# Attention logits of two graph-attention layers: the lookup matmuls in f32 instead of on three bf16 pieces

## The chip, the cores and the metric

The program runs on one core of one Trainium2 chip. The metric is the device time of one execution in microseconds (us); less is better. A profiled execution gives, beside its time, the start and length of every instruction on each engine: TensorE (PE for the matmuls, PEld for the loads of their stationary operand), VectorE (DVE), ScalarE (ACT), GpSimd (POOL) and SyncE (SP), and the clock that TensorE was granted, as a share of 2.4 GHz.

## The reference

The reference is a chain of four graph layers over 6250 nodes, 100000 edges and 128 features: a graph attention network of two attention layers, a GCN, a relational attention and a gated graph layer, each followed by a residual addition and a layer norm. What matters here is the score of an edge in each of the two attention layers:

```python
g = h @ W
s = (g * a_src).sum(-1)
d = (g * a_dst).sum(-1)
e = jax.nn.leaky_relu(s[src] + d[dst], NEG_SLOPE)
```

`s` and `d` are one number per node. For each edge, one of `s` must be looked up by its source and one of `d` by its destination, all in f32.

## The kernel before, in words

The nodes are stored as a table of 128 partitions by 52 columns (`NBP` = 52): node n lies in partition n mod 128 (its low digit) and in column n div 128 (its high digit). `scol` and `dcol` are the two tables `s` and `d` in that form, f32. The edges go in 196 groups (`GROUPS`) of 512 (`GE`), a group in 4 tiles (`GT`) of 128 edges.

`gat_logits(l)`, called once for each of the two layers, looks up both tables for all edges. For one group:

- ACT fetches the low digits of the group's destinations and sources as a row of bf16, spread over all partitions (`g_lo_rows`, L1075, a ring of 4).
- One-hots of the low digits, 128 partitions by 512 edges for each table: DVE makes that of the destinations with one comparison (`onehot`, L1108), ACT that of the sources with a Square and a Relu (L1081, L1083). They lie in `g_oh`, bf16, a ring of 4.
- PE multiplies, for each table and tile, the one-hot (stationary, 128x128) with the table (moving, 128x52): the row of 52 candidates of each edge (L1189). The table was split ahead into three bf16 pieces that add up to the f32 number (`g_parts`, L1150 and L1154), so there are 3 matmuls for each table and tile, added up in PSUM: 24 for a group. The result lies in one of two PSUM buffers (`g_psc`).
- DVE picks the candidate of the high digit: a comparison of a column number with the high digit (`match`, L1114), a product with the candidates (`take`, L1121), a sum over the 52 columns (`choose`, L1125), and the sum of both tables (`add`, L1129, into `tmp`).

The order is written out by hand. On DVE the step for group g is: one-hot of g+2, take of g+1, add of g, match of g+2, choose of g+1. PE waits, for a group, for both one-hots (`s_oh`, `s_oh2`) and until DVE has taken the group two before out of the same PSUM buffer (`s_take`). DVE and ACT wait with a one-hot of a ring place until PE is through with the group four before (`s_c`). ACT asks for the next digits after DVE's one-hot of the same ring place (`s_oh`).

Beside it, and with no data in common, POOL gathers rows of the layer's table by indirect DMA, four transfers for a group of edges (`keep_gathers`, L264), and SP loads their indices (L268) and stores them (L272). That is 78 groups' worth in layer 0 and 76 in layer 1 (`KEPT`), the rest being gathered in other stages. The stage ends when POOL, SP and the lookups are all through; then comes the softmax over the edges of a node.

Two other places in the kernel run f32 matmuls that the prediction reads: L706 makes the logit tables of layer 0 (a transposed block of `x`, 128x128, by two columns, `w_sd`), with the transposes of L700 between; L1626 is the weighted sum over the edges (a one-hot by 131 columns).

Of the kernel before, what the change touches and what calls it, by code (L numbers as in the profile page):

```python
# [24 lines left out]
BF16 = mybir.dt.bfloat16  # L25
ALU = mybir.AluOpType
# [3 lines left out]
P = 128  # L30
# [5 lines left out]
NBP = QUADS * 4  # L36
NPAD = NBP * P
GT = 4
GE = GT * P
# [11 lines left out]
RING = 4  # L51
# [37 lines left out]
def build(nc, A, out):  # L89
    top = ExitStack()  # L90
    with top:
        def sb(stack, name, shape, dt=F32):
            return stack.enter_context(nc.sbuf_tensor(name, shape, dt))

        def ps(stack, name, shape, dt=F32):
            return stack.enter_context(nc.psum_tensor(name, shape, dt))
# [3 lines left out]
        def sem(stack, name):  # L100
            s = stack.enter_context(nc.semaphore(name))
            used.append(s)
            return s

        @contextmanager
        def phase():

            with ExitStack() as st:
                used.clear()
                yield st  # L110
                with nc.Block() as block:
                    @block.gpsimd
                    def _(pool):
                        for s in used:
                            pool.sem_clear(s)
# [5 lines left out]
        acc = sb(top, "acc", [P, NBP * D + 8])  # L121
# [901 lines left out]
        def gat_logits(l):  # L1023
# [3 lines left out]


            with phase() as st:
                part = sb(st, f"g{l}_parts", [P, 2, 3, NBP], BF16)  # L1030
                rest = sb(st, f"g{l}_rest", [P, 2, NBP])
                trow = sb(st, f"g{l}_lo_rows", [P, RING, 2 * GE], BF16)
                oh = sb(st, f"g{l}_oh", [P, RING, 2 * GE], BF16)
                pid = sb(st, f"g{l}_pid", [P, 1])
                neg_pid = sb(st, f"g{l}_neg_pid", [P, 1])
                sq = acc[:, 0:2 * GE].rearrange("p (k e) -> p k e", k=2)
# [3 lines left out]
                u = tmp[:, 0:TILES]  # L1040
                ps_c = [ps(st, f"g{l}_psc{i}", [P, 2 * GT, 64]) for i in range(2)]
                s_pid = sem(st, f"g{l}_pid_ready")
                s_part = sem(st, f"g{l}_parts_ready")
                s_lo = [sem(st, f"g{l}_lo{k}") for k in range(RING)]
                s_oh = sem(st, f"g{l}_onehot_ready")
                s_oh2 = sem(st, f"g{l}_onehot2_ready")
# [9 lines left out]
                tabs = (dcol, scol)  # L1056
                with nc.Block() as block:
                    @block.gpsimd
                    def _(pool):
                        nc.gpsimd.iota(pid_i[:, :], pattern=[[0, 1]], base=0, channel_multiplier=1).then_inc(s_pid, 1)  # L1060
                        pool.wait_ge(s_pid, 1)
                        nc.gpsimd.tensor_copy(pid[:, :], pid_i[:, :]).then_inc(s_pid, 1)
                        pool.wait_ge(s_pid, 2)
                        keep_gathers(pool, gat_src(l), last - first, k_idx, k_land, k_st)
# [36 lines left out]
                    @block.vector  # L1101
                    def _(dve):
                        v = nc.vector

                        def onehot(g, k, r):
                            dve.wait_ge(s_lo[k % RING], r * 16 + 16)
                            dve.wait_ge(s_c, g + 1)
                            v.tensor_scalar(oh[:, k % RING, 0:GE], trow[:, k % RING, 0:GE], pid[:, :], None, ALU.is_equal).then_inc(s_oh, 1)  # L1108

                        def match(g, k):  # L1110

                            hi = hi_g[:, :, bass.ds(g * GT, GT)].unsqueeze(3).to_broadcast([P, 2, GT, NBP])
                            dve.wait_ge(s_pick, g + 1)
                            v.tensor_tensor(eq[:, k % 2, :, :, :], iota[:, 0:NBP].unsqueeze(1).unsqueeze(1).to_broadcast([P, 2, GT, NBP]), hi,  # L1114
                                            ALU.is_equal).then_inc(s_eq, 1)

                        def take(g, k):
                            cand = ps_c[k % 2][:, :, 0:NBP].rearrange("p (a t) b -> p a t b", a=2)
                            dve.wait_ge(s_c, g + 1 + RING)
                            dve.wait_ge(s_eq, g + 1)  # L1120
                            v.tensor_tensor(eq[:, k % 2, :, :, :], eq[:, k % 2, :, :, :], cand, ALU.mult).then_inc(s_take, 1)  # L1121

                        def choose(g, k):
                            dve.wait_ge(s_take, g + 3)
                            v.tensor_reduce(pick[:, k % 2, :, :], eq[:, k % 2, :, :, :], AX, ALU.add).then_inc(s_pick, 1)  # L1125

                        def add(g, k):
                            dve.wait_ge(s_pick, g + 3)
                            v.tensor_tensor(u[:, bass.ds(g * GT, GT)], pick[:, k % 2, 0, :], pick[:, k % 2, 1, :], ALU.add).then_inc(s_u, 1)  # L1129

                        def body(i, k, has):
                            g = i * RING + k
                            if has(2):
                                onehot(g + 2, k + 2, i + (k + 2) // RING)
                            if has(1):
                                take(g + 1, k + 1)
                            add(g, k)
                            if has(2):
                                match(g + 2, k + 2)
                            if has(1):  # L1140
                                dve.wait_ge(s_u, g + 1)
                                choose(g + 1, k + 1)

                        dve.sem_inc(s_take, 2)
                        dve.sem_inc(s_pick, 2)
                        n = 0
                        for a, tab in enumerate(tabs):
                            left = tab[:, :]
                            for i in range(3):
                                v.tensor_copy(part[:, a, i, :], left).then_inc(s_part, 1)  # L1150
                                n += 1
                                dve.wait_ge(s_part, n)
                                if i < 2:
                                    v.tensor_tensor(rest[:, a, :], left, part[:, a, i, :], ALU.subtract).then_inc(s_part, 1)  # L1154
                                    n += 1
                                    dve.wait_ge(s_part, n)
                                    left = rest[:, a, :]
                        dve.sem_inc(s_oh, RING)
                        dve.wait_ge(s_pid, 2)
                        for g in range(LEAD):  # L1160
                            onehot(g, g, 0)
                            match(g, g)
                        take(0, 0)
                        choose(0, 0)
                        whole = (GROUPS - LEAD) // RING
                        for i in range(0, whole):
                            for k in range(RING):
                                body(i, k, lambda d: True)
                        for g in range(whole * RING, GROUPS):
                            body(g // RING, g % RING, lambda d: g + d < GROUPS)  # L1170
                        dve.wait_ge(s_u, GROUPS)
                        v.tensor_copy(gx[:, 2, :], w_g[:, :]).then_inc(s_u, 1)
                        v.scalar_tensor_tensor(gx[:, 0, :], u[:, :], SLOPE, u[:, :], ALU.mult, ALU.max).then_inc(s_u, 1)
                        dve.wait_ge(s_u, GROUPS + 2)

                    @block.tensor
                    def _(pe):
                        pe.sem_inc(s_c, RING)
                        pe.wait_ge(s_part, 10)
                        for i in range(0, GROUPS // RING):  # L1180
                            for k in range(RING):
                                g = i * RING + k
                                pe.wait_ge(s_oh, g + 1 + RING)
                                pe.wait_ge(s_oh2, g + 1 + RING)
                                pe.wait_ge(s_take, g + 1)
                                for a in range(2):
                                    for t in range(GT):
                                        for n in range(3):
                                            m = nc.tensor.matmul(ps_c[k % 2][:, a * GT + t, 0:NBP], oh[:, k, a * GE + t * P:a * GE + (t + 1) * P],  # L1189
                                                                 part[:, a, n, :], start=(n == 0), stop=(n == 2))  # L1190
                                m.then_inc(s_c, 1)

        def segment_softmax(name, x, heads, last_max=None, aside=None, kept=None):
# [1605 lines left out]
        with ExitStack() as spare:  # L2799
            rest = sb(spare, "q_rest", [P, 2, 4, D])  # L2800
# [35 lines left out]
```

## Time and profile before

| what | value |
|---|---|
| median of 3 runs | 8215.74 us (8201.44 to 8236.54) |
| the profiled execution | 8222.3 us |
| its span, first to last instruction | 8220.5 us |
| mean granted TensorE clock | 0.654 of 2.4 GHz |
| busy in the span: PE, PEld | 4066.6 us (49%), 3274.5 us (40%) |
| busy in the span: DVE, ACT, POOL | 3569.6 us (43%), 1528.5 us (19%), 4158.7 us (51%) |
| L1189, matmuls / loads | x9408, 505.7 us / 439.3 us busy |

Durations of PE are those of a pipeline: instructions of one engine overlap, so the time that one of them costs is read from the distance of the starts or from the time of a run of them, not from its own duration. "issue" as a releaser is time in which an engine waited for nothing that the profile shows. The two stages at issue lie, from the span's start, at about 292 to 1082 us (layer 0) and 1756 to 2535 us (layer 1).

### The profile page before, as it was taken

To read this page: it belongs to the slowest core of one execution; us is meant where nothing else is said; L and a number is where in the kernel's file an instruction comes from. 1 tells how busy PE (TensorE), PEld (TensorE's weight loads), DVE (VectorE), ACT (ScalarE), POOL (GpSimd) and SP (SyncE) were. 2 spreads that over 40 slices of the span, in tenths; PEclk is the share of its full clock that TensorE was granted. 3 is DMA by queue.
4 is the path that set the end of the run, shared out by engine and by line. 5 is a ranking of instruction groups with operands and counts; after the bars stand their busy time and mean duration, and the time that the engine had idled before them with its cause. 6 is when DMAs were issued, how large, how long until landed. Compare 5 with 4: busy or idle time off the path is not lost. (4 is left out here: it accounts for less than half of the span.)

```text
span 8220.5 us, 107944 instructions
## 1 busy us (share of the span) xinstructions
PE 4066.6 (49%) x29332; PEld 3274.5 (40%) x29332; DVE 3569.6 (43%) x11001; ACT 1528.5 (19%) x3905; POOL 4158.7 (51%) x4416
## 2 busy tenths in 40 slices
PE   2403635430263532334444568888888474333446
PEld 1302525430253532333344445556666363233333
DVE  3004945430395532423333455555555792122224
ACT  0003710010272000200000133333333112000003
POOL 6473045547304566466565444455454435666660
PEclk7555557765555865655555678888888796555668
DMA  5233436533343654345555244444444461111110
GB/s 143 74 103 105 146 118 177 172 113 104 102 146 115 192 154 125 89 121 139 140 150 148 66 125 137 136 141 142 139 143 136 103 184 49 46 44 43 45 44 17
DMA packets 705868, 948.48 MB, mean 115 GB/s; under 512 B 263142, under 2 KB 367103, under 8 KB 704719
## 3 DMA queue, kind: packets, MB, share of 16 engines
q1 hardware_dynamic: 405027, 408.02, 16.6%
q0 software_dynamic: 140576, 316.92, 15.1%
q10 hardware_dynamic: 159712, 216.63, 8.6%
q8 instruction: 290, 4.75, 0.2%
q14 instruction: 263, 2.15, 0.1%
HBM read 705.34 MB, written 235.74 MB: 114 GB/s over the span
## 5 line engine op out<-in xcount | busy, mean ns | idle before, releaser
L2465 POOL DMA_INDIRECT s_rows<-rel_tab,s_idx x832 | 800.5, 962 | 792.0 <-issue 770.8
L264 POOL DMA_INDIRECT stash<-in_x,src_slot x784 | 796.2, 1016 | 760.4 <-DMA src_slot<-src_g 513.6
L264 POOL DMA_INDIRECT stash<-gat_tab,src_slot x784 | 788.1, 1005 | 757.1 <-DMA src_slot<-src_g 518.6
L1189 PE MATMUL g_psc<-g_parts,g_oh 128*128 128x52 bf16 x9408 | 505.7, 220 | 1066.7 <-issue 806.8
L959 POOL DMA_INDIRECT gcn_rows<-gcn_tab,src_slot x784 | 754.5, 962 | 494.3 <-issue 225.9
L959 POOL DMA_INDIRECT ggn_rows<-ggn_tab,src_slot x784 | 749.5, 956 | 441.0 <-issue 227.3
L1626 PE MATMUL e_psb<-tmp,e_oh 128*128 x3328 | 580.7, 340 | 783.5 <-DVE e_oh L1597 528.1
L1189 PEld LDWEIGHTS g_psc<-g_parts,g_oh 128*128 128x128 bf16 x9408 | 439.3, 120 | 1133.6 <-issue 854.4
L1626 PEld LDWEIGHTS e_psb<-tmp,e_oh 128*128 128x128 f32 x3328 | 524.1, 243 | 840.4 <-issue 840.1
L1959 PE MATMUL ggn_pso<-ggn_rows,ggn_oh 128*128 x1952 | 466.3, 397 | 663.2 <-DVE acc L1896 306.6
L2128 PE MATMUL gcn_pso<-gcn_rows,gcn_oh 128*128 x1952 | 500.1, 432 | 577.8 <-issue 398.9
L1959 PEld LDWEIGHTS ggn_pso<-ggn_rows,ggn_oh 128*128 128x128 f32 x1952 | 380.0, 281 | 750.0 <-issue 749.9
L2128 PEld LDWEIGHTS gcn_pso<-gcn_rows,gcn_oh 128*128 128x128 f32 x1952 | 423.6, 317 | 610.9 <-issue 610.3
L1121 DVE TENSOR_TENSOR g_eq<-g_eq,g_psc 128x416 f32<-128x416 f32 x392 | 231.6, 591 | 836.5 <-DMA src_slot<-src_g 412.3
L1896 DVE TENSOR_TENSOR acc<-acc,ggn_pso 128x128 f32 x244 | 69.9, 287 | 941.4 <-DMA s_oh<-oh_dram 623.8
L1081 ACT ACTIVATE acc<-g_lo_rows,g_neg_pid 128x512 f32<-128x512 bf16 x392 | 282.9, 722 | 1013.2 <-issue 810.2
L2072 DVE TENSOR_TENSOR acc<-acc,gcn_pso 128x128 f32 x244 | 70.1, 287 | 822.2 <-DMA src_slot<-src_g 543.3
L1595 DVE COPY tmp<-gx 128x12 f32<-128x12 f32 x392 | 74.6, 190 | 735.8 <-DMA e_values<-edge_v 306.0
L2597 PE MATMUL s_psk<-w_kv,s_msgT 128*128 128x128 f32 x1664 | 308.5, 342 | 0.0
L2537 DVE TENSOR_TENSOR tmp<-s_psk,tmp 128x512 f32<-128x512 f32 x208 | 143.1, 688 | 360.8 <-issue 311.7
L1597 DVE TENSOR_TENSOR e_oh<-iota,drel_v 128x512 f32<-128x512 f32 x416 | 284.6, 685 | 19.7 <-PE e_psb L1626 19.7
L2597 PEld LDWEIGHTS s_psk<-w_kv,s_msgT 128*128 128x128 f32 x1664 | 261.2, 239 | 62.2 <-issue 62.2
(499 smaller groups left out, 8373.5 us busy)
## 6 DMA issues: line engine op xcount, KB each, us to landing
edge_v<-stash SPq DMA_DIRECT2D x392, 256.0 KB
g_lo_rows<-lo_rows ACTq DMA_DIRECT2D x392, 256.0 KB
e_values<-edge_v SPq DMA_DIRECT2D x392, 256.0 KB
oh_dram<-tmp ACTq DMA_DIRECT2D x208, 256.0 KB
s_oh<-oh_dram SPq DMA_DIRECT2D x208, 256.0 KB
edge_v<-acc SPq DMA_DIRECT2D x208, 256.0 KB
r_values<-edge_v SPq DMA_DIRECT2D x208, 256.0 KB, 3.0
tmp<-drel_rows ACTq DMA_DIRECT2D x208, 128.0 KB
```

The source lines that it names most:

```text
L264: pool.indirect_dma_start(stash[:, k, t, :], None, tab[:, :], bass.IndirectOffsetOnAxis(ap=src_slot[:, k, t:t + 1], axis=0)).then_inc(s_la ...
L959: pool.indirect_dma_start(rows[:, k, t, :], None, tab[:, :], bass.IndirectOffsetOnAxis(ap=src_slot[:, k, t:t + 1], axis=0)).then_inc(s_row ...
L1081: nc.scalar.activation(sq[:, k % 2, :], trow[:, k, GE:2 * GE], ACT.Square, bias=neg_pid[:, :]).then_inc(s_sq, 1)
L1121: v.tensor_tensor(eq[:, k % 2, :, :, :], eq[:, k % 2, :, :, :], cand, ALU.mult).then_inc(s_take, 1)
L1189: m = nc.tensor.matmul(ps_c[k % 2][:, a * GT + t, 0:NBP], oh[:, k, a * GE + t * P:a * GE + (t + 1) * P], part[:, a, n, :], start=(n == 0), ...
L1597: v.tensor_tensor(oh[:, k % RING, :, :], iota[:, :].unsqueeze(1).to_broadcast([P, GT, P]), drel_v[:, bass.ds(n * GT, GT)].unsqueeze(2).to_ ...
L1626: nc.tensor.matmul(ps_b[:, bass.ds(bank, 1), 0:WCOLS].rearrange("p o d -> p (o d)"), oh[:, k, t, :], wv[:, bass.ds(slot, 1), :].rearrange( ...
L1959: m = nc.tensor.matmul(ps_o[k % 2][:, 0:D], oh[:, k % 2, t, :], rows[:, bass.ds(slot, 1), t, :].rearrange("p o d -> p (o d)"), start=(t == ...
L2128: m = mm(ps_o[k % 2][:, 0:D], oh[:, k % 2, t, :], rows[:, bass.ds(slot, 1), t, :].rearrange("p o d -> p (o d)"), start=(t == 0), stop=(t = ...
L2465: pool.indirect_dma_start(rows[:, k, t, :], None, rel_tab[:, :], bass.IndirectOffsetOnAxis(ap=idx[:, k, t:t + 1], axis=0)).then_inc(s_row[ ...
L2537: v.tensor_tensor(pq[:, :, :], ps_k[:, :, :], qe[:, :, :], ALU.mult).then_inc(s_pq, 1)
L2597: m = mm(ps_k[:, t, :], msgT[:, T[t]], w_kv[:, 0, :], start=False, stop=(t == GT - 1))
```

## The change

The tables are no longer split into pieces. `dcol` and `scol` themselves are the moving operand, in f32, and the one-hots are written in f32, into a part of the large buffer `acc` that is free in this stage. One matmul stands for each table and tile instead of three. The ten DVE instructions of the split and the wait of PE on them go.

```diff
-                part = sb(st, f"g{l}_parts", [P, 2, 3, NBP], BF16)
-                rest = sb(st, f"g{l}_rest", [P, 2, NBP])
                 trow = sb(st, f"g{l}_lo_rows", [P, RING, 2 * GE], BF16)
-                oh = sb(st, f"g{l}_oh", [P, RING, 2 * GE], BF16)
+                oh = acc[:, 2 * GE:(2 * RING + 2) * GE].rearrange("p (k e) -> p k e", k=RING)
...
-                s_part = sem(st, f"g{l}_parts_ready")
...
-                        n = 0
-                        for a, tab in enumerate(tabs):
-                            left = tab[:, :]
-                            for i in range(3):
-                                v.tensor_copy(part[:, a, i, :], left).then_inc(s_part, 1)
-                                n += 1
-                                dve.wait_ge(s_part, n)
-                                if i < 2:
-                                    v.tensor_tensor(rest[:, a, :], left, part[:, a, i, :], ALU.subtract).then_inc(s_part, 1)
-                                    n += 1
-                                    dve.wait_ge(s_part, n)
-                                    left = rest[:, a, :]
...
-                        pe.wait_ge(s_part, 10)
...
-                                        for n in range(3):
-                                            m = nc.tensor.matmul(ps_c[k % 2][:, a * GT + t, 0:NBP], oh[:, k, a * GE + t * P:a * GE + (t + 1) * P],
-                                                                 part[:, a, n, :], start=(n == 0), stop=(n == 2))
+                                        m = nc.tensor.matmul(ps_c[k % 2][:, a * GT + t, 0:NBP], oh[:, k, a * GE + t * P:a * GE + (t + 1) * P],
+                                                             tabs[a][:, :], start=True, stop=True)
```

## Rows read from the trace of the kernel before

**Rows 1.** Windows: length, busy us of PE, PEld, DVE, ACT, POOL; clock, DMA, GB/s.

```profile
737.00:1080.00 343.00, 224.22 (x4488) 203.29 (x4488) 342.93 (x939) 251.14 (x372) 0.00 (x0) 0.50 0.46 142
2200.00:2400.00 200.00, 130.84 (x2621) 118.68 (x2622) 200.00 (x548) 147.84 (x219) 0.00 (x0) 0.50 0.47 146
400.00:600.00 200.00, 11.37 (x70) 6.05 (x71) 6.11 (x15) 4.05 (x6) 151.75 (x151) 0.50 0.35 103
1160.00:1700.00 540.00, 273.40 (x1601) 248.66 (x1602) 265.24 (x595) 28.12 (x135) 304.40 (x296) 0.75 0.58 168
```

**Rows 2.** Timeline, layer 0, one group's cycle: start us, us, engine, line, instruction.

```profile
901.24 0.36 DVE L1108 TENSOR_SCALAR g_oh<-g_lo_rows,g_pid 128x512 bf16<-128x512 bf16 x1
...
901.73 1.20 PE L1189 MATMUL g_psc<-g_parts,g_oh 128*128 128x52 bf16 x24 [0.63 <-DVE g_oh L1108]
...
903.07 0.37 DVE L1108 TENSOR_SCALAR g_oh<-g_lo_rows,g_pid 128x512 bf16<-128x512 bf16 x1
```

**Rows 3.** Groups of instructions by line, 737.1 to 1080.1 us: count, busy us, mean ns.

```profile
L1081 ACT ACTIVATE acc<-g_lo_rows,g_neg_pid 128x512 f32<-128x512 bf16 x186 | 134.2, 722 | 104.1 <-DVE g_oh L1108 104.1
L1083 ACT ACTIVATE g_oh<-acc 128x512 bf16<-128x512 f32 x186 | 117.2, 630 | 5.9
...
L1121 DVE TENSOR_TENSOR g_eq<-g_eq,g_psc 128x416 f32<-128x416 f32 x188 | 111.6, 594 | 0.0
```

**Rows 4.** Groups of instructions by line, 2130 to 2532.5 us.

```profile
L1121 DVE TENSOR_TENSOR g_eq<-g_eq,g_psc 128x416 f32<-128x416 f32 x190 | 111.8, 588 | 73.8 <-DMA src_slot<-src_g 73.8
```

**Rows 5.** Timeline, layer 0, beside POOL's gathers.

```profile
374.39 0.39 PEld L1189 LDWEIGHTS g_psc<-g_parts,g_oh 128*128 128x128 bf16 x8 [24.82 <-issue]
...
376.57 0.10 PEld L1189 LDWEIGHTS g_psc<-g_parts,g_oh 128*128 128x128 bf16 x1 [1.79 <-issue]
...
378.00 0.20 PE L1189 MATMUL g_psc<-g_parts,g_oh 128*128 128x52 bf16 x1 [3.07 <-issue]
...
440.06 0.59 DVE L1121 TENSOR_TENSOR g_eq<-g_eq,g_psc 128x416 f32<-128x416 f32 x1 [65.72 <-remote]
...
710.57 0.59 DVE L1121 TENSOR_TENSOR g_eq<-g_eq,g_psc 128x416 f32<-128x416 f32 x1 [65.09 <-remote]
...
737.17 1.22 PE L1189 MATMUL g_psc<-g_parts,g_oh 128*128 128x52 bf16 x24 [1.71 <-DVE g_oh L1108]
```

**Rows 6.** One line, L264, 296 to 720 us: duration ns min/median/max, first and last start.

```profile
L264 POOL DMA_INDIRECT stash<-in_x,src_slot x311: 940/944/2591, 295.6 to 706.7; - x156
```

**Rows 7.** Line L706 (f32, two columns) in the timeline, and windows over it.

```profile
261.98 3.41 PE L706 MATMUL vt_psr<-w_sd,x_xT 128*128 128x2 f32 x16
...
237.00:240.00 3.00, 2.75 (x26) 2.68 (x26) 2.90 (x4) 1.35 (x3) 0.00 (x0) 1.00 0.46 95
...
248.00:252.00 4.00, 4.00 (x21) 4.00 (x22) 0.00 (x0) 0.70 (x2) 0.00 (x0) 0.50 0.01 4
```

**Rows 8.** Other f32 matmuls: line L706 and L1626 whole, and L1626 in the timeline.

```profile
L706 PE MATMUL vt_psr<-w_sd,x_xT 128*128 128x2 f32 x104 | 20.7, 322 | 0.2 <-ACT x_xT L747 0.2
...
L1768 PE MATMUL gcnt_psc<-w_gcn,gcnt_xT 128*128 128x128 f32 x104 | 23.6, 406 | 0.0
...
1311.47 2.06 PE L1626 MATMUL e_psb<-tmp,e_oh 128*128 x16 [1.20 <-issue]
...
1310.00:1320.00 10.00, 5.54 (x43) 4.80 (x41) 4.04 (x10) 0.63 (x3) 7.56 (x9) 1.00 0.77 225
```

**Rows 9.** DVE TENSOR_SCALAR of 512 columns, by line and form: busy us, mean ns.

```profile
L1108 DVE TENSOR_SCALAR g_oh<-g_lo_rows,g_pid 128x512 bf16<-128x512 bf16 x392 | 140.0, 357 | 3.1 <-DMA g_lo_rows<-lo_rows 3.1
...
L2227 DVE TENSOR_SCALAR gru_r<-gru_r 128x512 f32<-128x512 f32 x13 | 5.6, 427 | 68.0 <-ACT gru_z L2313 68.0
...
L471 DVE TENSOR_SCALAR tmp<-tmp,bv 128x512 f32<-128x512 f32 x2 | 1.3, 634 | 0.1
```

**Rows 10.** Timeline, start of the stage of layer 0.

```profile
294.12 0.19 DVE L1150 CAST g_parts<-g_rest 128x52 bf16<-128x52 f32 x1
...
295.79 0.35 DVE L1108 TENSOR_SCALAR g_oh<-g_lo_rows,g_pid 128x512 bf16<-128x512 bf16 x1 [1.48 <-DMA g_lo_rows<-lo_rows]
```

## The prediction

> **What bounds the kernel now.** I read the windows first, to see what each stage runs on. The logits stage has two parts. While POOL gathers, all compute engines nearly stand still: from 400 to 600 us PE is busy 11 us and DVE 6 us, POOL 152 us [rows 1]. Once POOL is through, DVE is busy all the time (342.9 of 343 us in layer 0, 200.0 of 200 us in layer 1), PE 65%, with TensorE at 0.50 of full clock, that is 1.2 GHz [rows 1].
>
> The timeline then gives the beat of the second part: DVE's one-hot starts at 901.24 and again at 903.07 us, 1.83 us for a group; PE's 24 matmuls take 1.20 us of it and 0.63 us go in waiting for DVE [rows 2]. ACT, with 0.72 and 0.63 us, has slack too [rows 3]. The groups by line count the groups: 188 takes in 343 us (1.824 us each) [rows 3] and 190 in layer 1 [rows 4]. So 378 of the 392 groups run at DVE's beat and 14 in the gather parts.
>
> In the gather part the timeline shows another beat: the take at 440.06 is followed by three more and that at 710.57 us, 67.6 us for a group [rows 5], while POOL issues 311 transfers in 411 us at a steady 0.94 us each [rows 6]. PE runs 8 weight loads at once, then one instruction about each 1.4 us (376.57, 378.00) with "issue" as the reason [rows 5]. What starves the engines there the profile doesn't name. That part is as long as POOL's gathers, which the change doesn't touch.
>
> **Part by part.**
>
> *The matmuls.* Removed: 24 bf16 matmuls for a group, 50 ns each (1.20/24) [rows 2]. Added: 8 f32 matmuls in the program. How many instructions is that? L706 multiplies 52 blocks, one matmul each, and shows x104 matmuls [rows 8]: two passes, each with its own weight load. So 16 passes for a group. What a pass costs with 52 moving columns no row shows; the nearest rows enclose it. At two columns, sixteen passes without a gap took 3.41 us at 1.2 GHz: 213 ns [rows 7]. With so few columns that is the price of loading 128 f32 weights. At 128 columns the mean is 23.6/104 = 227 ns at a clock that is mostly the low one [rows 8]. I take 213, since the two ends differ by 7% and the load fills the pass at either. So PE needs 16 x 0.213 = 3.41 us for a group, against 1.20 before and DVE's 1.83. The bound moves from DVE to PE.
>
> [...]
>
> *Does anything add a gap between groups?* PE waits for one-hot g and for the take of g-2. DVE does take g+1, add, match, choose and one-hot g+3 within one old beat, under 2.2 us, while PE is at group g+2 for 3.41 us. ACT's pair is about 1.4 us. Both run ahead, so PE should find its semaphores set. Bound: nothing at best; at worst 0.1 us for the three waits, +38 us over 378 groups. I take 0.
>
> *The clock.* Everything above holds at 1.2 GHz. The stage before never left it with PE 65% busy [rows 1]. Around L706 the clock was 1.00 as the two-column passes began and then fell to 0.50, with PE and PEld busy 4.00 of 4.00 us [rows 7]: passes that are mostly weight load didn't keep the clock up. The new passes move 2 x 52 columns in 213 ns; the old ones moved 24 x 52 in 1.83 us. At 1.2 GHz that is 16 x 104/1.2 = 1.39 us of 3.41, 41% of the time with columns in motion, against 24 x 52/1.2 = 1.04 us of 1.83, 57%. (That an f32 pass streams each column twice I take from the 128-column pass: 256/1.2 = 213 ns.) So less is moved per time than in a stage that stayed at 1.2 GHz. I take 0.50 throughout.
>
> *DVE's one-hot in f32.* 357 ns now; f32 rows of this size have 427 and 634 ns [rows 9], so +0.07 to +0.28 us, giving DVE 1.9 to 2.1 us. Covered by PE's 3.41; if PE ran at 2.4 GHz that cover is gone and it would count fully, some +0.14 us (nearer to 427, which like it has few operands). ACT's Relu writes f32 instead of bf16; L1081 writes f32 in 722 ns [rows 3], so +0.09 us at most, covered twice.
>
> *The split.* Ten DVE instructions end at 294.12 + 0.19 us, but the first one-hot waits for its DMA until 295.79 [rows 10]. Worth nothing: the digits are late anyway.
>
> *The gather part.* POOL's 411 us stay. What may move is how many groups get through beside it (7 in each layer) and the last slow group after it: DVE takes at 710.57, PE is back at full rate at 737.17 us [rows 5], some 27 us in which 24 pairs trickle. With 16 pairs, and 8 still quick, half of the slow ones go. Gain 0 to 20 us a layer, loss up to 10 if fewer groups pass beside POOL; I take 5 us a layer, -10 in all.
>
> **Sum.** 378 x (3.41 - 1.824) = +600 us, less 10: +590. The profiled execution took 8222.3 us, so 8812; it stood 6.6 us above the median, so 8806 us against 8215.7 (+7.2%).
>
> **Rivals.**
>
> *1. TensorE goes to 2.4 GHz, at times or all the time.* For it: PE will be busy without a break, and the f32 matmuls of 131 columns (L1626) run at a mean of 0.75 [rows 1]. Against: rows 7. At full clock a pass of L1626 cost 2.06/16 = 0.129 us [rows 8], fewer columns no more, so a group would be at most 2.06 us of PE and 1.97 of DVE: about 2.0, +0.18 x 378 = +68, 8274 us. At a mean of 0.75: 16 x 0.129/0.75 = 2.75, +350, about 8556 us. [...] Chance 0.13 for the mixed form, 0.04 for the full one.
>
> *2. The change doesn't do what two passes say:* the f32 matmul runs in one pass here. Then 8 x 0.213 = 1.71 us, DVE bounds at 1.97, +55 us, 8270 us. Against: every f32 matmul read shows two. Chance 0.02.
>
> *3. Faster: the starvation ends.* If what starves the engines beside POOL is the stream of PE's own instructions, a third fewer of them could let groups through beside the gathers. Place: 411 us in each layer. The stage took 784 us (296 to 1080) [rows 1, 10]; 196 groups at 3.41 are 668 us, if all ran beside POOL: -116 us a layer, 7984 us. It decides from the point where 3.41 n + (196 - n) x 3.41 + idle fits into 784 us: 108 groups after POOL's end fill the rest, so 88 must pass beside it, one in 4.7 us instead of 67. Against: DVE, whose instruction count barely changes, stands still just as long as PE. Chance 0.03.
>
> **How the numbers follow.** Forecast 0.78, rivals 0.13 + 0.04 + 0.02 + 0.03. Upwards the range takes the gap of 38 us and 10 us for the gather part: 8860. Downwards it takes the gather part (-30) and about half of the mixed clock, down to a mean near 0.6, where a group costs about 2.9 us: 8620. Left out are the rest of rival 1 and rivals 2 and 3, under 0.2. 0.5% is about what a measurement of this kernel can tell from no change, 41 us: faster 0.03, same 0.01, slower 0.96.
>
> **What the changed profile would show.** L1189 x6272 instead of x9408, f32, with as many weight loads; in the part without gathers PE busy all the time, DVE waiting for `g_psc` over 1 us a group, takes 3.41 us apart, the clock at 0.50. The gather part ends at the same time and the stages are some 295 us longer each; nothing else moves. A clock above 0.6 in these stages, or takes less than 2.5 us apart, would make the prediction wrong; so would takes 10 us apart beside POOL.

## The result and the profile after

The changed kernel took 8807.73 us (median, 8791.56 to 8808.34); the kernel before took 8209.15 us (8201.44 to 8236.54) beside it. The ratio is 1.0718, 95% interval 1.0689 to 1.0747: slower by 7%. The profiled execution took 8807.3 us, 585 more than that of before. On another chip of the same sort the pair came out at 1.0708 (run `after_again` below).

First the windows of the changed kernel: a stretch beside the gathers, one after them in layer 0, one in layer 1 (length, busy us of PE, PEld, DVE, ACT, POOL; clock, DMA, GB/s).

```profile
400.00:600.00 200.00, 14.62 (x64) 13.95 (x64) 9.12 (x20) 5.40 (x8) 152.19 (x152) 0.50 0.36 104
800.00:1000.00 200.00, 200.00 (x939) 200.00 (x939) 120.03 (x293) 79.73 (x118) 0.00 (x0) 0.50 0.24 78
2500.00:2900.00 400.00, 400.00 (x1877) 400.00 (x1877) 240.49 (x587) 158.12 (x234) 0.00 (x0) 0.50 0.26 78
```

The second and third lines answer to [rows 1]. Before, DVE was busy all the time and PE 65%; now PE and PEld are busy without a break and DVE 60%. The clock is 0.50 as before. 939 passes in 200 us are 213 ns each, and 1877 in 400 us are the same.

The timeline of one group's cycle answers to [rows 2].

```profile
899.77 1.91 PE L1172 MATMUL g_psc<-dcol,acc 128*128 128x52 f32 x8
900.02 0.59 DVE L1118 TENSOR_TENSOR g_eq<-g_eq,g_psc 128x416 f32<-128x416 f32 x1 [1.36 <-PE g_psc L1172]
...
901.48 1.91 PE L1172 MATMUL g_psc<-scol,acc 128*128 128x52 f32 x8
901.59 0.48 DVE L1105 TENSOR_SCALAR acc<-g_lo_rows,g_pid 128x512 f32<-128x512 bf16 x1
...
903.43 0.59 DVE L1118 TENSOR_TENSOR g_eq<-g_eq,g_psc 128x416 f32<-128x416 f32 x1 [1.36 <-PE g_psc L1172]
```

Eight passes for one table, eight for the other, and the next take 3.41 us after the last. PE has no gap; DVE waits 1.36 us for `g_psc` in each cycle. The f32 one-hot takes 0.48 us instead of 0.36.

The page's groups of instructions (busy us, mean ns, idle before and its releaser):

```profile
L1172 PE MATMUL g_psc<-dcol,acc 128*128 128x52 f32 x3136 | 749.7, 417 | 797.3 <-issue 725.9
L1172 PEld LDWEIGHTS g_psc<-dcol,acc 128*128 128x128 f32 x3136 | 714.8, 333 | 801.8 <-issue 740.9
L1118 DVE TENSOR_TENSOR g_eq<-g_eq,g_psc 128x416 f32<-128x416 f32 x392 | 230.3, 588 | 1318.8 <-PE g_psc L1172 501.6
L1172 PE MATMUL g_psc<-scol,acc 128*128 128x52 f32 x3136 | 748.9, 417 | 0.0
```

3136 matmuls for each table are 16 passes for each of 392 groups, where the program has 8 matmuls. DVE's take now has 501.6 us of waiting for PE ahead of it; in the stretches without gathers it had none [rows 3].

Beside the gathers something moved that the prediction had at 5 us a layer. DVE's takes there:

```profile
423.38 0.59 DVE L1118 TENSOR_TENSOR g_eq<-g_eq,g_psc 128x416 f32<-128x416 f32 x1 [42.99 <-remote]
...
468.57 0.59 DVE L1118 TENSOR_TENSOR g_eq<-g_eq,g_psc 128x416 f32<-128x416 f32 x1 [42.96 <-remote]
...
513.71 0.59 DVE L1118 TENSOR_TENSOR g_eq<-g_eq,g_psc 128x416 f32<-128x416 f32 x1 [42.91 <-remote]
```

They are 45.2 us apart, against 67.6 before [rows 5]. That is 2/3, the ratio of the numbers of PE instructions in a group (32 against 48), and it let 3 more groups through in layer 0 and 4 in layer 1 (the last of these four lies in the changeover, 2.0 us behind the one before).

**Where the time went.** Counted in both traces, 188 takes of each layer came at full rate before, and 185 and 184 after. The 376 groups cost 3.41 - 1.826 us more each, +596; 7 groups that passed in the shadow of the gathers save 7 x 3.41 = 24. That is +572. Measured: the copy behind the lookups of layer 0 starts 285.7 us later (1365.74 against 1080.06), the last sum of layer 1 starts 571.6 us later (3103.9 against 2532.3). The remaining 13 us of the 585 appear behind the two stages. No instruction there changed, and their cause wasn't looked for; single executions of the kernel before differ by 35 us.

### The profile page after: what moved, and what is told of

It reads as the page before. It is cut to its first block and busy times, and to the rows that moved or that the text cites. A ratio compares the mean times of both kernels' runs of the same rounds, so it can differ in the third digit from the quotient of the medians.

```text
span 8805.4 us, 101648 instructions
## 1 busy us (share of the span) xinstructions
PE 4896.4 (56%) x26196; PEld 4166.4 (47%) x26196; DVE 3654.9 (42%) x10981; ACT 1529.6 (17%) x3905; POOL 4157.2 (47%) x4416
## 5 line engine op out<-in xcount | busy, mean ns | idle before, releaser
L264 POOL DMA_INDIRECT stash<-gat_tab,src_slot x784 | 788.6, 1006 | 1050.9 <-DMA src_slot<-src_g 809.6
L264 POOL DMA_INDIRECT stash<-in_x,src_slot x784 | 795.6, 1015 | 1030.8 <-DMA src_slot<-src_g 785.8
L1172 PE MATMUL g_psc<-dcol,acc 128*128 128x52 f32 x3136 | 749.7, 417 | 797.3 <-issue 725.9
L1172 PEld LDWEIGHTS g_psc<-dcol,acc 128*128 128x128 f32 x3136 | 714.8, 333 | 801.8 <-issue 740.9
L1118 DVE TENSOR_TENSOR g_eq<-g_eq,g_psc 128x416 f32<-128x416 f32 x392 | 230.3, 588 | 1318.8 <-PE g_psc L1172 501.6
L1172 PE MATMUL g_psc<-scol,acc 128*128 128x52 f32 x3136 | 748.9, 417 | 0.0
L1172 PEld LDWEIGHTS g_psc<-scol,acc 128*128 128x128 f32 x3136 | 715.9, 333 | 0.0
```

The source lines that it names most:

```text
L264: pool.indirect_dma_start(stash[:, k, t, :], None, tab[:, :], bass.IndirectOffsetOnAxis(ap=src_slot[:, k, t:t + 1], axis=0)).then_inc(s_la ...
```

## Experiments

The first set of experiments ran on a chip on which the kernel before takes 6109 us instead of 8209, with no standing still beside the gathers: a quick chip, below. The next two sets ran on chips like that of the prediction (8166 and 8179 us; a slow chip, below), and the last again on a quick chip (6114 us). So each result is told with the time of the kernel before in the same set, and a ratio is always within one set.

**1. Is a pass bound by its weight load?** The changed kernel, its matmuls moving 2 columns instead of 52.

```diff
-                                        m = nc.tensor.matmul(ps_c[k % 2][:, a * GT + t, 0:NBP], oh[:, k, a * GE + t * P:a * GE + (t + 1) * P],
-                                                             tabs[a][:, :], start=True, stop=True)
+                                        m = nc.tensor.matmul(ps_c[k % 2][:, a * GT + t, 0:2], oh[:, k, a * GE + t * P:a * GE + (t + 1) * P],
+                                                             tabs[a][:, 0:2], start=True, stop=True)
```

> The kernel after the change, but each f32 matmul of the lookups moves 2 of the table's 52 columns (the other 50 candidates are left at zero, so that part of the lookup is left out; PSUM is cleared once before). Weight-load theory (a pass costs the load of 128 f32 weights, 213 ns at 1.2 GHz, whatever the columns up to 104): takes stay 3.41 us apart in the part without gathers, and the time stays at 8808 us within 15. Rival, the moving columns set the pass: takes come near DVE's own beat of about 2.0 us, and some 530 us go. Clock 0.50 in both.

Kernel before 6109.26 us there, this one 6670.02; ratio 1.0911 (1.0879 to 1.0942). Its window, which lies beside the gathers:

```profile
300.00:500.00 200.00, 200.00 (x939) 200.00 (x939) 124.34 (x295) 78.97 (x117) 152.39 (x157) 0.50 0.65 181
```

939 passes in 200 us, as with 52 columns, so from 2 to 52 the columns cost nothing at this clock. What is left to set the pass is the weight load, which PEld shows busy for all 200 us. The forecast of 8808 us belonged to a slow chip and wasn't tested here. The line also shows something new: on this chip PE runs at full rate while POOL gathers (152 of 200 us).

**2. One bf16 piece, 8 matmuls for a group.** The kernel before with one of its three pieces.

```diff
-                                        for n in range(3):
+                                        for n in range(1):
...
-                                                                 part[:, a, n, :], start=(n == 0), stop=(n == 2))
+                                                                 part[:, a, n, :], start=True, stop=True)
```

> The kernel before, but with the first of the three bf16 pieces alone (pieces 2 and 3 are left out of the product): 8 bf16 matmuls for a group instead of 24. DVE-bound theory: in the part without gathers takes stay 1.82 us apart, since PE's 24 matmuls had 0.63 us of slack; that part gives nothing. Gather-part theory (there the beat is 1.4 us for each PE instruction: 48 gave 67.6 us, 32 gave 45.2): 16 instructions give about 23 us for a group, so some 18 groups instead of 7 pass beside POOL, 11 x 1.82 = 20 us a layer, and the slow tail shrinks by some 10 us: in all about 55 to 65 us faster than before. Rival (the beat in the gather part hangs on DVE or on POOL and only by chance followed PE): beat stays 45 to 67 us and the time is within 20 us of before.

6110.58 us against 6109.26, ratio 1.0004 (0.9993 to 1.0016). No gain: in its trace the lookups aren't starved here (the takes are at most 2.0 us apart, the last at 593.7 us) and POOL's gathers go on without a break past that. The same kernel on a slow chip:

> The kernel with the first bf16 piece alone once more (pieces 2 and 3 are left out), for a chip of the other kind. Where the lookups stand still beside POOL's gathers: the beat there is 1.41 us for each of PE's instructions as in three kernels so far (48: 67.6, 32: 45.2, 16: 22.7), so 16 give about 22.6 us, 18 groups instead of 7 pass beside POOL, the tail shrinks, and the time falls by 45 to 65 us against before; the beat without gathers stays 1.82 us. On a chip of the kind of 6109 us: no change again.

8104.26 us against 8179.49, ratio 0.9908 (0.9879 to 0.9937): 75 us less, where 45 to 65 were expected. Its windows, beside the gathers and after them, and its takes beside them:

```profile
400.00:600.00 200.00, 4.75 (x72) 3.51 (x72) 17.45 (x45) 12.15 (x18) 148.40 (x151) 0.50 0.39 110
800.00:1000.00 200.00, 55.09 (x872) 42.93 (x872) 200.00 (x549) 148.06 (x220) 0.00 (x0) 0.50 0.46 145
```

```profile
434.47 0.59 DVE L1121 TENSOR_TENSOR g_eq<-g_eq,g_psc 128x416 f32<-128x416 f32 x1 [21.01 <-issue]
...
502.36 0.59 DVE L1121 TENSOR_TENSOR g_eq<-g_eq,g_psc 128x416 f32<-128x416 f32 x1 [20.72 <-remote]
```

After the gathers nothing changed: DVE is busy 200.00 us, and two thirds of PE's work gone are worth nothing. Beside them three takes came in 67.9 us, one in 22.6, a third of 67.6 for a third of PE's instructions. In layer 0, 21 takes came before full rate instead of 8, and the lookups ended 24 us earlier (1056.0 against 1080.1 us in the trace of before), as 13 groups at 1.83 us give; layer 1 did about the same. That is some 50 of the 75 us; where the rest lies isn't known, since no execution of the kernel before was profiled on that chip.

**3. No gathers beside the lookups.** The kernel before; POOL starts its gathers when all 196 groups are summed.

```diff
+                        pool.wait_ge(s_u, GROUPS)
                         keep_gathers(pool, gat_src(l), last - first, k_idx, k_land, k_st)
```

> The kernel before, but POOL begins its gathers of this stage when the last lookup is through (it waits for all 196 sums). Theory that POOL's gathers starve PE: all 196 groups run at 1.83 us, 359 us, and then the gathers take their 411 us: the stage has about 775 us instead of 784, the total falls by some 10 to 25 us. Rival (the slow start belongs to the stage itself, such as its instruction stream or its row loads): the first groups are again 67 us apart without any gather beside them, and the total rises by 350 us or more a layer.

On the quick chip 6823.55 us in a single execution, 714 more than before: two stretches that lay beside each other now come one after the other. The time is near the rival's, its reason isn't: the takes are 1.82 us apart from the first on.

> The kernel before with POOL's gathers of the stage after the last lookup, once more, for a chip of the other kind. If the gathers are what slows PE: all 196 groups at 1.83 us from the start, then 411 us of gathers, the stage about 775 us and the total 10 to 25 us less than before. If PE is slow there without gathers too: takes 67 us apart at the start, and the total rises by 350 us or more a layer. On a chip of 6109 us: 6824 us again.

On a slow chip 8158.41 us against 8179.49, in a single execution: nothing lost. The windows there:

```profile
400.00:600.00 200.00, 131.25 (x2631) 119.15 (x2632) 200.00 (x549) 147.69 (x220) 0.00 (x0) 0.50 0.47 145
737.00:860.00 123.00, 0.00 (x0) 0.00 (x0) 0.00 (x0) 0.00 (x0) 92.75 (x98) 0.50 0.35 104
```

Against the third of [rows 1], the same 200 us hold 2631 matmuls instead of 70. So it is the stream of gathers (with the index loads and stores that SP does for them, which moved too) that starves PE, and on such a chip running the lookups beside gathers that come one right after the other is worth next to nothing.

**4. The gathers paced.** The kernel before; gather j of a layer waits until 2.5 j groups are summed.

```diff
+                if pace is not None and j > 0:
+                    pool.wait_ge(pace, j * 5 // 2)
                 pool.sem_inc(s_turn, 1)
...
-                        keep_gathers(pool, gat_src(l), last - first, k_idx, k_land, k_st)
+                        keep_gathers(pool, gat_src(l), last - first, k_idx, k_land, k_st, pace=s_u)
```

> The kernel before, but POOL's gather j of this stage waits until 2.5 j groups have been looked up. If gathers one right after the other starve PE, and pauses let it catch up, both go on together: a stage near 420 to 500 us instead of 784, 550 us or more in all. If every gather costs PE the same stall, whenever it comes, nothing is gained: each gather still holds PE for about 5 us, the stage stays at 784 us or is longer, up to 850. If PE, once slow, stays slow until POOL has been quiet for some 25 us (as after the last gather), the stage would be far longer, over 1000 us.

Quick chip: 6117.69 us against 6109.26, ratio 1.0013 (1.0001 to 1.0024).

> The kernel before with POOL's gather j held until 2.5 j groups have been looked up, once more, for a chip of the other kind. Theory that gathers one right after the other slow PE and that pauses let it recover: the stage falls from 784 to 420 to 500 us a layer. Theory that PE stays slow as long as there are gathers at any pace: the lookups get 67 us a group while gathers are left, each gather waits for 2.5 groups, and the stage becomes many times as long. Theory that the slowness drains at a fixed rate after each gather (the 26 us after the last one): something between, over 784 us. On a chip of 6109 us: no change again.

Slow chip, one execution: 7891.27 us against 8179.49, 288 us less than the kernel before, and the quickest of all kernels on a slow chip. DVE's takes in its timeline in layer 0, four at full rate before gathers interrupt:

```profile
504.26 0.59 DVE L1123 TENSOR_TENSOR g_eq<-g_eq,g_psc 128x416 f32<-128x416 f32 x1 [6.04 <-remote]
...
506.10 0.58 DVE L1123 TENSOR_TENSOR g_eq<-g_eq,g_psc 128x416 f32<-128x416 f32 x1
...
507.93 0.58 DVE L1123 TENSOR_TENSOR g_eq<-g_eq,g_psc 128x416 f32<-128x416 f32 x1
...
509.75 0.58 DVE L1123 TENSOR_TENSOR g_eq<-g_eq,g_psc 128x416 f32<-128x416 f32 x1
...
512.99 0.59 DVE L1123 TENSOR_TENSOR g_eq<-g_eq,g_psc 128x416 f32<-128x416 f32 x1 [1.15 <-remote]
```

The next take comes at 520.92 us: five groups in 16.7 us, with the two gathers of four transfers that go with them. The stage took 644 us (291 to 935), where it took 784. None of the theories had that: it lies between the 420 to 500 us of the first and the 784 and more of the others. Gathers alone (411 us) and lookups alone (359 us) add up to 770, so paced they overlap by some 125 us, and unpaced hardly at all. To put an interval to the time, the kernel ran once more:

> The kernel of before with gather j of a layer waiting until 2.5 j groups are summed, once more and now timed in rounds, to give the single look (7891 us against 8179 of the kernel before) an interval. Theory (each of TensorE's instructions waits while a gather is in progress and none is lost while GpSimd waits for the lookups): on a chip where the kernel before takes about 8,170 us, 7,890 us, a ratio of 0.965, within 0.5% of it in each round. Rival (the single look was an outlier, pacing only shifts the standing still to another place): 0.995 to 1.005. On a chip where the kernel before takes 6,109 us, both say 1.00.

This time it was a quick chip: 6125.42 us against 6113.74, ratio 1.0013 (1.0004 to 1.0023), as in the first set. So the gain on slow chips rests on one execution without an interval, though 288 us is 15 times the spread of the three runs of the kernel before beside it (8170.09 to 8189.00). Both kinds of chip, same program, same window:

The quick one (`e4_paced_timed`):

```profile
400.00:600.00 200.00, 123.47 (x2448) 110.70 (x2448) 197.55 (x516) 136.20 (x202) 152.21 (x157) 0.50 0.82 236
```

The slow one (`e4_paced_b`):

```profile
400.00:600.00 200.00, 84.12 (x1444) 68.37 (x1443) 114.12 (x300) 81.11 (x120) 93.01 (x98) 0.50 0.49 145
```

**5. The changed kernel again, on a second chip.** No edit.

> The kernel after the change, unaltered, on a chip where the lookups have so far not stood still beside POOL's gathers (the kernel before took 6109 us there). Weight-load theory: with two columns a group took 3.41 us and the stage 196 x 3.41 = 669 us beside the gathers, against about 400 us of the kernel before, where POOL's own 390 us set the end; so the total is 6109 + 2 x 270 = about 6650 us, the 6670 of the two-column kernel within 20. If the standing still of the first pair of profiles belonged to the kernel and not to the chip or the time, takes of 45 us would be seen again.

8746.17 us against 8166.25, ratio 1.0708 (1.0678 to 1.0738). This was a slow chip, so the forecast of 6650 us wasn't tested. Takes 45 us apart beside the gathers were there again, and 3.41 us apart after them: the first pair of profiles is repeated on a second chip.

**6. More columns for each weight load.** The changed kernel with both tables side by side as the moving operand, 104 columns; the take is split in two.

```diff
-                ps_c = [ps(st, f"g{l}_psc{i}", [P, 2 * GT, 64]) for i in range(2)]
+                ps_c = [ps(st, f"g{l}_psc{i}", [P, 2 * GT, 128]) for i in range(2)]
+                both = sb(st, f"g{l}_both", [P, 2 * NBP])
...
-                            v.tensor_tensor(eq[:, k % 2, :, :, :], eq[:, k % 2, :, :, :], cand, ALU.mult).then_inc(s_take, 1)
+                            v.tensor_tensor(eq[:, k % 2, 0, :, :], eq[:, k % 2, 0, :, :], ps_c[k % 2][:, 0:GT, 0:NBP], ALU.mult)
+                            v.tensor_tensor(eq[:, k % 2, 1, :, :], eq[:, k % 2, 1, :, :], ps_c[k % 2][:, GT:2 * GT, NBP:2 * NBP], ALU.mult).then_inc(s_take, 1)
...
-                                                             tabs[a][:, :], start=True, stop=True)
+                                                             both[:, :], start=True, stop=True)
```

> The kernel after the change, but every f32 matmul moves both tables side by side (104 columns; of each one-hot's product the half of the other table is not read), and the take is split in two instructions. Low-clock theory (the loss is the f32 weight load at 1.2 GHz, and the clock stays low because few columns are moved beside it): the 104 columns fit under the same 213 ns, the clock rises to 1.00 for most of the stage, a pass falls to about 107 ns, and the beat becomes DVE's, about 2.0 to 2.1 us; on the chip of 6109 us the total is 6110 to 6180 us. Rival 1, the weight load costs 213 ns at either clock: the clock rises but the beat stays 3.41 us, 6650 us. Rival 2, the clock stays at 0.50: the beat stays 3.41 us, 6650 us.

8270.32 us against 8166.25, ratio 1.0116 (1.0084 to 1.0149), 476 us less than the changed kernel in the same set, though each matmul moves twice as much. Its windows and its timeline:

```profile
400.00:600.00 200.00, 14.96 (x64) 13.95 (x64) 8.85 (x24) 5.40 (x8) 151.07 (x151) 0.51 0.36 104
800.00:1000.00 200.00, 191.52 (x1513) 175.59 (x1511) 195.56 (x567) 127.72 (x189) 0.00 (x0) 1.00 0.41 125
```

```profile
901.32 0.37 DVE L1119 TENSOR_TENSOR g_eq<-g_eq,g_psc 128x208 f32<-128x208 f32 x1
901.45 1.86 PEld L1177 LDWEIGHTS g_psc<-g_both,acc 128*128 128x128 f32 x16 [0.35 <-DVE acc L1107]
...
903.48 1.64 PEld L1177 LDWEIGHTS g_psc<-g_both,acc 128*128 128x128 f32 x14 [0.17 <-DVE acc L1107]
903.52 0.37 DVE L1119 TENSOR_TENSOR g_eq<-g_eq,g_psc 128x208 f32<-128x208 f32 x1
```

The clock is 1.00, 16 loads take 1.86 us instead of 3.4 (the pass is cut to some 0.12 us, 0.107 expected), and the groups come 2.12 us apart (1513 passes in 200 us). DVE is again the engine that bounds (195.6 of 200 us). Beside the gathers nothing changed against the kernel after: 64 matmuls in 200 us in both, so the columns don't matter there. Of the clock this says nothing, since it was 0.51 in that stretch, as in the kernel after.

Whether it was the layout or the columns, the next one tells (`e7_half_columns`): the same layout, 52 columns.

```diff
-                                        m = nc.tensor.matmul(ps_c[k % 2][:, a * GT + t, 0:2 * NBP], oh[:, k, a * GE + t * P:a * GE + (t + 1) * P],
-                                                             both[:, :], start=True, stop=True)
+                                        m = nc.tensor.matmul(ps_c[k % 2][:, a * GT + t, a * NBP:(a + 1) * NBP], oh[:, k, a * GE + t * P:a * GE + (t + 1) * P],
+                                                             both[:, a * NBP:(a + 1) * NBP], start=True, stop=True)
```

> The control of the kernel with both tables side by side: its PSUM layout, its joined table and its two takes, but each f32 matmul again moves the 52 columns of its own table, so nothing but the number of moved columns differs. If the columns raised the clock there: clock 0.50, takes 3.41 us apart in the part without gathers, and the time of the kernel after the change within 15 us (ratio to before 1.07 on a chip of 8166 us, 1.09 on one of 6109 us). If the layout or the split take did it: clock 1.00 and takes 2.1 us apart.

8738.77 us against 8179.49, ratio 1.0684 (1.0643 to 1.0724). Window:

```profile
800.00:1000.00 200.00, 200.00 (x940) 200.00 (x939) 123.46 (x351) 79.21 (x118) 0.00 (x0) 0.50 0.26 77
```

Back at 0.50 and 213 ns a pass. The two kernels differ in the moved columns alone, so it was these that raised the clock.

**7. Half of the f32 passes.** The changed kernel with the matmuls of one table alone (`for a in range(1)`).

> The kernel after the change, but only the destinations' table is looked up: 4 f32 matmuls, 8 passes, for a group (the sources' half of PSUM is cleared once, and that lookup is left out). PE needs 8 x 0.213 = 1.71 us, so DVE bounds: this measures its beat with the f32 one-hot. Expected 1.83 + 0.12 = 1.95 us (the one-hot took 476 ns instead of 357), clock 0.50, the stage about 395 us, set as much by POOL as by DVE, and a total of about 6115 us on the chip of 6109 us. Rival: if reading f32 weights out of the same buffer that DVE and ACT write slows these, the beat is over 2.2 us.

One execution: 8183.85 us against 8166.25. Windows:

```profile
400.00:600.00 200.00, 17.55 (x72) 16.04 (x72) 18.72 (x45) 12.15 (x18) 150.99 (x150) 0.50 0.38 110
800.00:1000.00 200.00, 190.37 (x783) 173.93 (x783) 196.40 (x489) 131.94 (x196) 0.00 (x0) 0.50 0.42 129
```

783 passes in 200 us are 2.04 us a group: with PE's work halved, DVE bounds again (196.4 of 200), 0.1 us above the 1.95 that its instructions alone would give. That is between the theory and its rival (over 2.2 us), and what takes the 0.1 us isn't shown. Beside the gathers the numbers of PE instructions and DVE's (x72, x45) are those of the bf16 kernel of experiment 2 (x72, x45): the type of the operands doesn't matter there, only how many instructions.

## Why the prediction was right, and where it was off

**Two passes for each f32 matmul, 213 ns each:** right, to the nanosecond, in both layers (939 and 1877 passes), and the run with 2 columns (939 passes in 200 us as well) shows that it isn't the columns that set it. The step of the prediction that chose the two-column row over the 227 ns of the wider one is what made the forecast good. The group takes 3.41 us, 16 passes of 213 ns.

**No gap between groups:** right. PE is busy 200.00 of 200.00 us; of the bound of 38 us nothing came. DVE's take, add, match, choose and one-hot run from 900.02 to 902.07 us, 2.05 us of the cycle of 3.41 (the prediction had under 2.2), and ACT's pair from 902.53 to 903.91, 1.38 us (about 1.4). From 800 to 1000 us the trace has no wait of PE for either; DVE waits 59 times for PE, 1.36 us each.

**The clock stays at 0.50:** right, and it was the largest risk, as experiment 6 shows: at 1.00 the same 16 passes left DVE as the bound, with 2.12 us a group, and the loss was 1.2% instead of 7.1%. So most of what the change costs is the f32 load at 1.2 GHz; 476 of 580 us went when the clock rose. The prediction took from the 128-column pass that an f32 pass streams each column twice. That row can't show it, since a pass of two columns took 213 ns too. Other rows of the same trace bear it out: with the clock at 0.50 the two passes of 512 columns of L2282 start at 8058.77 and 8059.62 us, 0.85 us apart, 1.66 ns for a column, which is two cycles of 1.2 GHz; with the clock at 1.00 the f32 passes of 512 columns in L2282 to L2284 start 0.43 us apart (two each from 8061.11, 8061.97 and 8062.83 us), 0.84 ns for a column, two cycles of 2.4 GHz. And the bf16 passes of L1189 in that stage take one cycle for a column, as the prediction's 24 x 52/1.2 has it: 24 of them take 1.20 us and the last 3 of a group 0.31 (900.79 to 901.10), so they follow each other at 0.042 us, 0.81 ns for each of the 52 columns (a cycle is 0.83). Rival 1 in its full form forecast 2.0 us a group, 68 us more on the lookups, 8274 us in all on the chip of the prediction. Experiment 6 has 2.12 us, and 104 us more than the kernel before in its set. The nearness of its 8270 us to the 8274 is chance, since that kernel before took 8166 us and not 8216. Of the 0.12 us that a group took longer, the split take can account for most (2 x 0.37 us instead of 0.59). So the rival's price was somewhat low, and its condition wasn't met. What rival 1 had for it, PE busy without a break, did come: the windows show it busy for all of 200 and 400 us, at 0.50.

**DVE's one-hot in f32:** 476 ns, +0.12 us, inside the bounds of 0.07 to 0.28, somewhat above the 427 ns row that the prediction leaned to. Covered by PE's 3.41 us, as it said.

**The split:** worth nothing, as forecast. The first take of layer 0 comes at 305.1 us against 307.3 before, 2.2 us that fall in the stretch where PE crawls anyway.

**The gather part:** the term that was mis-sized. "I take 5 us a layer, -10 in all": it was 3 and 4 more groups, 7 x 3.41 = 24 us. The step behind it had only the tail after the gathers in mind, which didn't shrink (full rate begins at 736.8 us, 737.0 before), and left the beat beside them at 67.6 us; it fell to 45.2 us. Together with two groups too many in the count of full-rate groups (378 for 376) the sum comes to 572 us where the prediction had 590, and 13 us elsewhere bring the profiled difference to 585. The errors partly cancel; the 1.7 us between the forecast of 8806 and the median is luck.

**The argument against rival 3 was wrong.** It said that DVE stands still just as long as PE although its instruction count barely changes, so the count can't be what matters. But a take can't start before PE is through with its group, so DVE stands still with PE whatever its own count is (the profile has only "remote" ahead of the takes). The beat follows the number of PE's instructions:

```
matmul and load pairs in a group      24 (before)   16 (after)   8 (one piece)
us from take to take beside gathers   67.6          45.2         22.6
us for a pair                         2.82          2.83         2.83
```

The rival's mechanism was half there: fewer instructions do let more groups through, in proportion. Its price needed 88 groups beside POOL, one in 4.7 us, where proportion gives one in 45. The low chance was right for another reason than the one given.

**"The stages are some 295 us longer each; nothing else moves":** they were 286 us longer, and the rest held to 13 us. **"Takes 10 us apart beside POOL"** didn't come, on this sort of chip.

## What to carry to other kernels

Replacing three bf16 matmuls by one in f32 isn't a third of the work. Each f32 matmul was two passes of 213 ns at 1.2 GHz, 426 ns where three bf16 matmuls of the same shape took 150. A pass took the same 213 ns with 2 moved columns and with 52, while the engine that loads the stationary operand was busy for all of the 200 us, so count passes and loads in a row of the trace before believing the count in the source. Where such a chain must be, try more columns for each load: here the same passes with 104 instead of 52 ran at the full clock, and the group fell from 3.41 to 2.12 us. And a stage that overlaps two streams should be tried with one of them held back: pacing the gathers was worth 288 us in one execution on a chip where they starve TensorE, and cost 0.13% on one where they don't.

## What was unexpected of the hardware

**The same program takes 6109 us on one chip and 8166 to 8209 us on others.** The gathers are as quick on both (152 transfers in 200 us beside 157, 0.94 us each), but where it takes 8166 us or more TensorE gets one instruction each 1.41 us while they run (67.6/48), whatever its type or columns (from 400 to 600 us 64 matmuls in f32 with 52 columns and with 104, 72 in bf16 and in f32 with one table), and it stays slow after the last gather: for 29 us before the change (its instruction ends at 707.74 us, full rate begins at 737.0) and 27 after it (710.14, 736.8). With the gathers held back the lookups run at 1.83 us from the start. What in the chip does this stays open; the profile says only "issue". It isn't a lack of DMA bandwidth at that moment: from 715 to 735 us of the kernel before POOL is idle and the core's DMA engines move nothing (0.00 busy, 0 GB/s), and PE still gets only 11 matmuls and 12 loads. How instructions reach TensorE, which no view shows and no run varied, stays a rival untested. The two logits stages hold only some 770 of the 2057 us between the two sorts of chip (784 us each against about 400); where the others lie wasn't looked into. Whether it belongs to the chip or to its state isn't settled either: two sets of runs that gave the same chip number had 8179 and 6114 us. On the quick sort the changed kernel itself wasn't run; its two-column form, with the same beat of 3.41 us, lost 9% there.

**TensorE busy without a break stayed at half its clock.** With 52 columns behind each f32 load it was at 0.50, busy for all of 400 us; with 104, and PE busy 96%, it was at 1.00; with 52 in the same layout at 0.50 again.
